# State-space layers of a hybrid kernel: products on another engine, a split on TensorE, a new order of the unit

## The reference

```python
h = rmsnorm(x); u, z = split(h @ in_w)
uc = silu(causal_conv4(u) + cb)
dt_r, Bm, Cm = split(uc @ xp_w)
dt = softplus(dt_r @ dt_w + dt_b); A = -exp(A_log)
# scan over the 256 steps
h = exp(dt_t[..., None] * A) * h + (dt_t * u_t)[..., None] * B_t[:, None, :]
y_t = einsum('bds,bs->bd', h, C_t)
y = (y + uc * Dp) * silu(z)
x = x + y @ out_w
```

## Time and profile before

| | before |
|---|---|
| median of 3 runs | 411.38 us (409.92 to 411.42) |
| span of the profiled execution | 409.9 us |
| TensorE, VectorE busy | 340.5, 314.7 us |
| ScalarE, GpSimd busy | 249.1, 210.6 us |

### The profile page before, as it was taken

One profiled execution on the slowest core, in us unless ns is written; L12 is line 12 of the kernel. 1 busy time (PEld: TensorE's weight loads), 2 busy tenths in 40 slices (PEclk: granted clock), 3 DMA queues, 4 the chain that ended last, 5 costly groups with the idle time before them and its releaser, 6 DMA issues.

```text
span 409.9 us, 5884 instructions
## 1 busy us (share of the span) xinstructions
PE 340.5 (83%) x1818; PEld 235.1 (57%) x1818; DVE 314.7 (77%) x538; ACT 249.1 (61%) x681; POOL 210.6 (51%) x235
## 2 busy tenths in 40 slices
PE   5868998999899986888887979888888879768674
PEld 3356765565584654566664757566566647557442
DVE  2674678898653618779999799979988999998653
ACT  2012378888727455948778586948676786862170
POOL 1985000000000028788889698868977797882000
PEclk9985999999979997899999899899989999987868
DMA  7900000000002105142450515161342326050000
GB/s 238 403 7 1 2 1 2 0 2 2 0 2 64 40 4 206 44 165 75 173 178 31 208 43 205 29 220 62 144 162 86 123 86 210 3 203 0 2 0 13
DMA packets 11345, 35.24 MB, mean 86 GB/s; under 512 B 2368, under 2 KB 2992, under 8 KB 11192
## 3 DMA queue, kind: packets, MB, share of 16 engines
q1 hardware_dynamic: 11032, 34.61, 23.9%
q10 hardware_dynamic: 288, 0.33, 0.3%
HBM read 34.54 MB, written 0.39 MB: 85 GB/s over the span
## 4 chain that ended last, share of the span: by engine, by line
PE 53%; DVE 24%; ACT 12%; issue 5%; DMA 3%; POOL 2%; DVEq 0%; SPq 0%; POOLq 0%; ACTq 0%
PE PS L664 15%; DVE big L1133 7%; ACT PS L1405 4%; PE PS L511 4%; PE PS L643 3%; DVE big L1121 3%; DVE big L1140 3%; PE PS L475 2%; ACT sg L1368 2%; PE PS L289 2%; PE PS L295 2%; PE PS L627 2%; PE PS L405 2%; PE PS L575 2%; PE PS L485 2%
## 5 line engine op out<-in xcount | busy, mean ns | idle before, releaser
L1133 DVE TENSOR_TENSOR_SCAN big<-PS,big 128x1024 f32<-128x1024 f32 x48 | 109.3, 2284 | 3.0 <-ACT PS L1405 2.7
L664 PE MATMUL PS<-big,cst 128*128 128x256 f32 x384 | 96.0, 407 | 0.0
L1405 ACT ACTIVATE PS<-dt,amat 128x255 f32<-128x255 f32 x192 | 80.1, 466 | 25.4 <-DVE dt L1105 21.5
L1611 POOL TENSOR_TENSOR big<-dtu,big 128x1024 f32<-128x1024 f32 x36 | 84.2, 2356 | 7.2 <-DVE dtu L1108 6.6
L664 PEld LDWEIGHTS PS<-big,cst 128*128 128x128 f32 x384 | 76.8, 205 | 14.9 <-issue 3.7
L1644 POOL TENSOR_SCALAR lnv<-mv 128x4 f32<-128x4 f32 x1 | 0.4, 418 | 93.9 <-DVE mv L770 93.9
L1140 DVE TENSOR_TENSOR big<-big,PS 128x1024 f32<-128x1024 f32 x36 | 43.8, 1216 | 0.9
L1239 ACT ACTIVATE big<-PS 128x512 f32<-128x512 f32 (+1 forms) x43 | 24.8, 584 | 22.3 <-PE PS L511 7.3
L643 PE MATMUL PS<-stack,pick_b 96*128 96x256 bf16 x144 | 23.9, 292 | 17.0 <-DVE big L1140 9.2
L1286 ACT ACTIVATE big<-PS,big 128x256 f32<-128x256 f32 x64 | 29.8, 475 | 1.5 <-DVE big L902 1.5
L1619 POOL TENSOR_TENSOR big<-big 128x1024 f32<-128x1024 f32 x12 | 28.3, 2358 | 1.1 <-DVE big L1133 1.1
(11 more groups left out here) (309 smaller groups left out, 624.6 us busy)
## 6 DMA issues: line engine op xcount, KB each, us to landing
big<-spill SPq DMA_DIRECT2D x48, 512.0 KB, 5.6
wmt<-in_wm SPq DMA_DIRECT2D x6, 418.0 KB, 3.2
w3t<-in_w SPq DMA_DIRECT2D x1, 1588.0 KB, 13.5
big<-routed SPq DMA_DIRECT2D x8, 128.0 KB, 3.0
w2t<-in_w SPq DMA_DIRECT2D x1, 896.0 KB, 10.1
cst<-in_const SPq DMA_DIRECT2D x1, 848.0 KB, 8.0
w5t<-in_w SPq DMA_DIRECT2D x1, 812.0 KB, 15.0
w1t<-in_w SPq DMA_DIRECT2D x1, 385.0 KB, 8.4
```

The source lines that it names most:

```text
L664: last = pe.matmul(yps, ident, hc[:, g, s], start=False, stop=(g == NSG - 1 and s == SG - 1))
L1133: v.tensor_tensor_scan(flat(hst[g][:]), flat(da[g % 2]), flat(dbu[:, g]), 0.0, ALU.mult, ALU.add).then_inc(sem("m_h"), 1)
L1405: one = act.activation(da[g % 2][:, n, 1:N], dt[b][:, 1:N], ACT.Exp, scale=amat[k][:, col:col + 1])
L1611: pool.tensor_tensor(dbu[:, g], dtu[b][:].unsqueeze(1).to_broadcast([P, SG, N]), bsp[b][:, SG * (g - 1):SG * g], ALU.mult).then_inc(sem("m ...
```

## The change

The state-space part is rewritten.

- Groups 0 and 1 of dbu are made on VectorE and groups 2 and 3 on GpSimd; groups 0, 1 and 2 of hc on GpSimd and group 3 on VectorE, in two halves. Five of the eight products are thus on GpSimd, where four were.
- The spreads are three a unit instead of four: B of groups 0 and 1, and C of group 3. SyncE brings five tiles of 512 KB a unit instead of four.
- The split: ScalarE copies the high part from PSUM to `stack`, TensorE subtracts it in PSUM (`split_hi`, weights -2 * identity), ScalarE copies the middle part, TensorE subtracts again (`split_mid`), ScalarE copies the low part.
- The biases are added by bfloat16 matmuls of K = 96; sigmoid(u) is (1 + tanh)/2 with the half moved into later scales; z is copied first and its tanh taken at the end of the preparation; dt_w and x_proj are multiplied together once, ahead of the loop, on TensorE, so that dt comes from uc in one matmul.
- The softplus uses another polynomial form: Abs, Exp, Tanh and three Square on ACT, three operations on DVE.
- The residual is added on TensorE (identity times Y into `hidp`) and copied to Y by ScalarE (`keep_residual`); norm and hs read `hidp`.
- The transposes write both halves of the partitions, the lower one shifted by one column, so that `prep_ht` is one ACT copy.
- All weights of the six layers are loaded and prepared ahead; `keep_awake` is only used ahead of unit 0; the loops are written out for all 12 units.
- In the order of TensorE, the sums of groups 0, 1, 2 and 3 of a unit all stand behind `split_hi` of the next unit.

The core of the diff:

```diff
             for u in range(UNITS):
-                n, b = u // 2 + 1, u % 2
-                if b == 1 and 2 <= n < NL:
...
-                sp.wait_ge(sem("m_xds"), u + 1)
-                sp.dma_start(spill[b], xds[b][SG:DS + 2 * SG, :]).then_inc(sem("st_B"), 16)
+                sp.wait_ge(sem("m_xs"), 4 * u + 1)
+                sp.dma_start(spill[b], xds[b][2 * SG:7 * SG, :]).then_inc(sem("st_B"), 16)
...
+            pe.wait_ge(sem("ld_wr"), 32)
+            for n in range(NL):
+                last = pe.transpose(PS[0:RANK, 4 + n // 4, (n % 4) * P:(n % 4 + 1) * P], wr[:, n], ident)
...
-            spare(7, 2)
+            for n in range(NL):
+                last = pe.matmul(PS[:, 7 - n // 2, N + (n % 2) * P:N + (n % 2 + 1) * P], wrT[:, n], dtw[:, n],
+                                 start=True, stop=True)
+            last.then_inc(sem("m_wp"), 1)
             to_T2(X, PS[:, 3, 0:N], "ln_out", 2, "turned")
+            pe.wait_ge(sem("m_wdt"), 3)
             spare(7, 1)
...
+            def split_hi(u):
+                pe.wait_ge(sem("m_xs"), 4 * u + 2)
+                pe.wait_ge(sem("m_sp"), 6 * u + 1)
+                pe.matmul(xd[0:32], less_hi[64:96], stack[u % 2][64:96], start=False, stop=False)
+                pe.matmul(xd[32:64], less_hi[64:96], stack[u % 2][64:96], start=False, stop=True).then_inc(sem("m_less"), 1)
+            def split_mid(u):
+                pe.wait_ge(sem("m_xs"), 4 * u + 3)
+                pe.matmul(xd[0:32], less_mid[32:64], stack[u % 2][32:64], start=False, stop=True).then_inc(sem("m_less"), 1)
...
+            for u in range(UNITS):
+                more = u + 1 < UNITS
+                if u:
+                    sum_y(u - 1, 2)
+                    sum_last(u - 1)
+                spread_first(u)
+                if u:
+                    out_proj(u - 1)
+                spread_second(u)
+                if more:
+                    prep_transpose(u + 1)
+                    prep_in(u + 1)
+                spread_last(u)
+                if more:
+                    prep_x(u + 1)
+                sum_skip(u, u + 1 if more else None)
+                if more:
+                    split_hi(u + 1)
+                sum_y(u, 0)
+                if more:
+                    split_mid(u + 1)
+                sum_y(u, 1)
```

The list of VectorE:

```diff
+            for u in range(UNITS):
+                prep_dt(u)
+                if u:
+                    gate(u - 1)
+                drive(u, 0)
+                scan(u, 0)
+                drive(u, 1)
+                scan(u, 1)
+                if u + 1 < UNITS:
+                    prep_uc(u + 1)
+                scan(u, 2)
+                scan(u, 3)
+                weigh_last(u)
```

ScalarE's copies, for which the split waits:

```diff
+            def prep_xd(u):
+                act.wait_ge(sem("m_xd"), 2 * u + 2)
+                act.activation(xds[u % 2][:], xd[64:96], ACT.Copy, scale=0.5).then_inc(sem("m_xs"), 1)
+                act.activation(stack[u % 2][64:96], xd[64:96], ACT.Copy, scale=0.5).then_inc(sem("m_xs"), 1)
+            def prep_softplus(u):
+                act.activation(sp_a, dtp, ACT.Abs).then_inc(sem("m_sp"), 1)
```

The list of GpSimd:

```diff
+            for u in range(UNITS):
+                drive(u, 2)
+                if more:
+                    prep_rms(u + 1)
+                drive(u, 3)
+                for g in range(3):
+                    weigh(u, g)
+                if more:
+                    prep_gz(u + 1)
```

More of the change, by code:

```diff
@@ new lines, in sum_y, with sum_last @@
+            def sum_y(u, g):
+                pe.wait_ge(sem("m_hc"), 3 * u + g + 1)
+                for s in range(SG):
+                    pe.matmul(yps, ident, hc[:, g, s], start=False, stop=False)
+            def sum_last(u):
+                for h in range(2):
+                    pe.wait_ge(sem("m_hc3"), 2 * u + h + 1)
+                    for s in range(2 * h, 2 * h + 2):
+                        last = pe.matmul(yps, ident, hc[:, NSG - 1, s], start=False, stop=(s == SG - 1))
+                last.then_inc(sem("m_y"), 1)
@@ L714, in _ @@
+            keep_awake(3)
+            prep_x(0)
             keep_awake(1)
-            prep_dt(0, 0, 0)
+            split_hi(0)
+            keep_awake(1)
+            split_mid(0)
             keep_awake(5)
-            pe_step(0, 0, first=True)
-            with pe.Fori(0, 2) as i:
-                for s in range(1, 5):
-                    pe_step(i, s)
-            for s in range(9, 12):
-                pe_step(0, s, last=(s == 11))
-            sum_y(UNITS - 1, 1, NSG - 1)
-            out_proj(UNITS - 1, 1, 1)
+            for u in range(UNITS):
[20 more added lines that the diff above has]
+                sum_y(u, 1)
@@ L1142, in _, with drive @@
-            prep_uc(0, 0, 0)
-            v_step(0, 0, first=True)
-            with v.Fori(0, 2) as i:
-                for s in range(1, 5):
-                    v_step(i, s)
-            for s in range(9, 12):
-                v_step(0, s, last=(s == 11))
+                v.tensor_tensor(yg[u % 2], yps, gz[u % 2], ALU.mult).then_inc(sem("m_gate"), 1)
+            def drive(u, g):
+                v.wait_ge(sem("m_BC"), 3 * u + g + 1)
+                if g == 0:
+                    v.wait_ge(sem("m_dtu"), u + 1)
+                v.tensor_tensor(dbu[:, g], dtu[u % 2].unsqueeze(1).to_broadcast([P, SG, N]), BCv, ALU.mult)\
+                    .then_inc(sem("m_dbu"), 1)
@@ L1437, in _, with prep_norm @@
[L1437 to L1447 removed]
+            def prep_norm(u):
+                b = u % 2
+                for a in range(HALF):
+                    last = act.activation(sqs[:, a], hidp[:, a] if u >= 2 else Y[:, a, b], ACT.Square, scale=D ** -0.5,
+                                          accum_out=ssq[b][:, a:a + 1])
+                last.then_inc(sem("m_ssq"), 1)
@@ new lines, in decay @@
+            def decay(u, g, some):
+                if some[0] == 0:
+                    act.wait_ge(sem("m_dt"), u + 1)
+                    if u or g >= 2:
+                        act.wait_ge(sem("m_h"), u * NSG + g - 1)
+                for n in some:
+                    col = SG * g + n
+                    one = act.activation(da[g % 2][:, n, 1:N], dt[u % 2][:, 1:N], ACT.Exp, scale=amat[:, u // 2, col:col + 1])
+                if some[-1] == SG - 1:
+                    one.then_inc(sem("m_da"), 1)
```

672 lines of the change are left out of this document (293 added, 379 removed).

## The result

The changed kernel takes 463.08 us (median of 4 runs, 455.79 to 476.14) against 410.69 (409.92 to 411.42) for the kernel before: a ratio of 1.118, with a 95% interval of 1.109 to 1.127. The ratio is taken over the executions that lie within 1.5% of a kernel's fastest, here 455.79 and 462.55. The forecast was 428.4, range 404 to 446. Its sign was right; the time lies 17 us above the range. The profiled execution took 463.61 with a span of 461.8, which is 51.9 more than before.

What follows compares the result with a forecast made beforehand. TensorE's sum was taken to end each round, with its clock adding time. Span 409.9 + 14.6 (ten rounds) + 2.5 (start and end) = 427.0, plus 1.4 for the median, gave 428.4 us, range 404 to 446.

Steps and rivals of the forecast that it cites:

- What bounds the kernel: Unit loop: TensorE's sum ends each round, VectorE nearly as late; after the change VectorE idles 2.7 us before the gate.
- Steps 1 to 5: Unit round at full clock, laid out from the previous sum's end to the sixteen products' end: 18.4 us against 17.8.
- The clock term: Unit rounds: at least one TensorE clock fall in each, 1.5 us a round, bounds 0.2 and 3.5.
- steps 2 and 3: Round's early part: out projection, norm, transposes, ht, projection, tanh to 7.0 us; then TensorE's x stage to 9.85.
- step 1: Round's start on VectorE: gate, two B drives, two scans to 7.60 us, then uc to 8.10, covering step 2's chain.
- Around the rounds: Before the units, unit 0's start and the end: together +2.5 us, bounds -2 and +8, GpSimd's prologue work 1.5 of it.
- The sum: Whole kernel: 409.9 + 14.6 + 2.5 = 427.0 us of span, plus 1.4 for the runs' median, 428.4.
- rival (d): VectorE and GpSimd take turns for whole instructions: +2.0 us a round, 447 us; chance 0.05.
- The rule weighed: Shared SBUF ports: VectorE with two SBUF inputs and GpSimd wait out each other's whole instruction; speaks against the change.
- (a): VectorE sets the rounds, 15.8 or 16.1 us each: 391 us, chance 0.12; another 0.08 for part of it (400 to 409).
- (b): The clock holds in the unit rounds, 18.6 us each: 415.5 us; chance 0.14.
- (c): Two clock falls on the sum in every round, 21.9 us each: 448 us; chance 0.10.

Runs made afterwards that it cites:

- the run with three idle matmuls: The changed kernel with three idle matmuls a unit put back between the second spread and the transposes: 424.67 us, ratio 1.038.
- the three other kernels with the same prologue: The changed kernel with three idle matmuls (424.67 us), with sums of groups 0 and 1 ahead of the two splits (443.34), and with both (414.86).
- the changed kernel with the best of the edits: The changed kernel with three idle matmuls, groups 0 and 1 summed ahead of the splits, GpSimd's prologue work in 256-column pieces behind the attention: 410.70 us, ratio 0.997.
- the kernel before with two fillers: The kernel before plus one zero-adding matmul ahead of the x projection and one ahead of the dt projection, each unit: 404.22 us, ratio 0.986.
- the early sum: The changed kernel with a unit's first four products ahead of split_hi and the next four ahead of split_mid, nothing else: 443.34 us, ratio 1.084.

## Why the prediction was right and wrong

**What bounds the kernel.** Right. TensorE's sum ends every round, VectorE waits 2.76 us ahead of each gate (predicted 2.7), and GpSimd is busy 13.4 us a round (13.5).

**Steps 1 to 5, the undisturbed round.** Right within half a microsecond. The kernel after never showed it, but the run with three idle matmuls did: 18.83 against 18.4. The first product came at 11.31 (predicted 11.35). The sixteen products with the split between them took 7.5 instead of 7.0, since in this order a matmul takes 0.456 us (7.30 / 16) and not 0.432.

**The clock term.** This is the first step that failed: in the prediction's words "I take 1.5 a round". "At least one fall in every round" was right, and it was traced to the right edit. Its price was not 1.5 but 3.3 (22.15 - 18.83). I priced a fall "about 0.5 to 0.9 where it doubles three or four matmuls of steps 2 and 3". At 0.43 each that is 1.3 to 1.7, of which step 1 could cover 0.6. And in the round shown it doubled eleven: with L630 ahead of them they take 7.0 us on the chain, 266.63 to 273.61, and at full clock 4.1 (270.05 to 274.11). The other price, 1.75, came from the earlier trace rows, a fall that lasts 3.4 us in the trace of the kernel before, under a busy TensorE. Here it lasted 6.8 us in five rounds, 10.2 in four and 13.7 in one. The error was to price a fall by the matmuls that I thought it would meet and not by its length, which one row of a fuller stage cannot bound. The kernel before without its idle matmuls bears the larger price out: 20.42 against the 17.8 of its rounds without a fall. In ten rounds +37.1 came where +14.6 was predicted, 22.5 of the 35 us by which the forecast is off. Why the clock stays down longer in one round than in the next is open.

**Around the rounds.** This failed too: +2.5 was predicted for start and end together, +14.9 came. The term for GpSimd's prologue work was "0 to 6 us, and I take 1.5, as most of them would have to meet it". In the profile of the kernel after 10.5 us were lost up to the first exponential, most of them in that very way: the steps of VectorE at 37 to 47 us had 9.5 us where they needed 1.7. In the three other kernels with the same prologue the loss up to there is 6.7 to 10.1. I had counted the operations that meet GpSimd, each by a row in which the wait was for the rest of a 0.73 us instruction; here the instructions that they meet are 3.1 us long. Of the rest of the +16.4, 3.1 come up to the columns, where the clock fell once more, and 2.5 from the router's end to the first sum. These are in part luck: with the same code up to the columns they start 6.7 us late in one profile and 13.6 in another.

**The sum.** Two slips in it change nothing: rival (d), +2.0 a round on the forecast, is 448 and not 447. And 1.4 us were added on the reading that the span stands at the lowest run; in the runs here the time of an execution is 1.8 us above its own span (463.61 and 461.8).

**The rule weighed.** It stood beside the earlier trace rows and priced rival (d). The Trainium skill, page "SBUF — State Buffer", section "SBUF: two separate sides", has the engine that comes second wait for the whole of the other's instruction. The trace agrees: 3.14 us beside 3.09, 1.57 beside 1.57, and 0.77 when the instructions were cut to a sixth. I had applied it to the rounds alone, as rival (d), where it cost nothing: GpSimd's products there mean 2.35 and 2.37 us as before, and VectorE's three steps meet at most a 0.73 us one (L1124 takes 0.90 beside it instead of 0.42, inside the 2.76 us of waiting).

**The rivals.** (a) and (b) are out. (c) has the size, 21.9 against 22.15, and not the mechanism: not two falls on the sum but one long one, on the projection and the x stage, which reaches the sum only in the last round. (d) is out for the rounds and right at the start.

**What remains of the change.** With the clock held in the rounds of both, the changed kernel with the best of the edits takes 410.7 and the kernel before with two fillers 404.2; the rounds are 18.02 and 17.93. The work that went from VectorE to GpSimd is real: VectorE is busy 158.0 us in the ten rounds where it was 170.0, and the 2.76 us by which it waits are the yield. Nothing made the chain through a round shorter, and with the early sum that chain runs through VectorE's two scans ahead of uc.

## What to carry to other kernels

Before taking filler matmuls out, look at what TensorE does in the microseconds around them, and price a fall of the clock by the whole stretch behind it, not by the one row at hand. A filler has a duration like any other matmul, 0.43 us here: put it into the wait just ahead of the place where the clock falls, and no longer than that wait. Work handed to GpSimd is cut into pieces and put where VectorE is idle, for VectorE waited out each instruction that it met. The two together gained 4 us here; pieces alone gained nothing that could be told, and whole instructions in the idle place were not tried. Look also at how far the same code varies from profile to profile before a gain at the start is put down to an edit.

## What the runs showed that I had not expected

- A stretch at 0.50 was 3.4 us long in the rounds of the kernel before and 6.8 to 13.7 us in those of the kernel after, although TensorE was busy without a gap for most of it (268 to 273: 5.00 of 5.00 us).
- VectorE's operations with one tensor input and a scalar column wait for GpSimd as well: a pair of TENSOR_SCALAR of 256 columns took 3.99 us instead of 0.62. So does a SCALAR_TENSOR_TENSOR of a single column (L891), 1.75 us instead of 0.22.
- Adding 0.9 us of filler a round at the old place (five for three idle matmuls) made the kernel before 8 us longer; adding 0.9 us at two others made it 6 us shorter.
- The start of a kernel with unchanged code differs by up to 7 us between profiles, by where the clock falls.
